# A transformer block with a mixture of experts: the third pair of expert weights is loaded behind the scatters, results are copied out later

## The chip, the cores and the metric

The kernel runs on one core of one Trainium2 chip. The metric is the device time of one execution, in microseconds (us), as the median of several runs. A profile of one execution tells what each engine and each transfer did.

## The reference

`x` has 4 sequences of 128 tokens of 512 numbers, so 512 tokens in all. Three parts are added to it one after the other: cross attention over 4 x 2048 context tokens, self attention, and the mixture of experts. Only the last one is touched here:

```python
logits = rn @ gate_w.T                       # rn: normalised tokens, 8 experts
probs = softmax(logits); rw, sel = top_k(probs, 2)
comb = sum(one_hot(sel, 8) * rw[..., None], axis=1)
h = gelu(einsum('nc,efc->enf', xf, w1))      # w1: 8 x 1024 x 512
y = einsum('enf,ecf->enc', h, w2)            # w2: 8 x 512 x 1024
out = einsum('enc,ne->nc', y, comb)
```

Each token needs two of the eight experts. The output is `x` plus this sum.

## The kernel before, in words

Cross attention takes the first two thirds of the time, self attention ends at about 809 us, and `mixture` does the rest.

**Tiles.** The 1024 pairs (token, expert) are sorted into tiles of 128 rows that belong to one expert each. There are 15 tiles (`TILES`): tile k below 8 has expert k, and the 7 further ones have the expert that the routing gives them (`of_tile`, read by `experts_of_further_tiles` on the sync engine, SP, by way of registers). Each tile loads its expert's two matrices anew, 2 MB each.

**Scatter of rows.** GpSimd (POOL) writes records of 514 numbers (512 of the normalised token, its weight, its token number) to the places of the sorted order in `slots_in` in HBM. These are 8 indirect DMAs (L1494): four from `t.normed` (first choices), four from `m_second` (second choices). Only when all 8 have landed (`sent`) may SP load tiles of rows back (`rows_load`, L1462). The first three tiles (`EARLY`) take their activations by another way, straight from SBUF (`rows_picked`), so they need no scatter, but the weight of a row, by which a result is scaled, comes with the loaded rows also for them.

**One tile k.** ScalarE (ACT) splits each f32 matrix into a high half in f16 (`w1_high` L1654, `w2_high` L1662, two instructions each), VectorE (DVE) makes the low half from the matrix and the high half, both in SBUF (`w1_low` L1622, `w2_low` L1629, two each). TensorE (PE) does `up` (L1797 to L1799, 96 products of 128x128), ACT applies Gelu (L1713) and splits (L1717), DVE makes the low half of that (L1638), PE does `down_tile` (L1779 to L1781, 24 products of 128x512), ACT scales the result into `y` (`y_evict`, L1680), and POOL adds `y` to the output by an indirect DMA with addition (L1504). POOL waits there for `y_out` of tile k and for the landing of the addition before it (`y_added`).

**Order of the work.** It is written out by hand, engine by engine. ACT in its iteration k: `y_evict(k - 2)`, Gelu and split of both halves of tile k, `x_high(k + 1)`, `w2_high(k)`, `w1_high(k + 2)`; after the last iteration the results of tiles 13 and 14. DVE in iteration k: `w1_low(k + 1)`, the low halves of tile k, `x_low(k + 1)`, `w2_low(k)`. PE: `up(k)`, transposes of the rows of k + 1, `down_tile(k - 1)`. SP's queue: `w1_load(2)`, `w1_load(3)`, `w2_load(2)`, the wait for `sent`, four `rows_load`, the experts of the further tiles, and then for each k `rows_load(k + 4)`, `w1_load(k + 3)`, `w2_load(k + 2)`.

**Buffers.** There are two buffers for each matrix (raw f32, high, low), so a matrix is loaded when the low half of the one two before it is done. `rows_in` is a ring of 8 (`ROWS_RING`); a slot comes free when the addition of its tile has landed. `y` has two buffers, `ps_y` (in PSUM) two.

Of the kernel before, what the change touches and what calls it, by code (L numbers as in the profile page):

```python
# [14 lines left out]
ALU, ACT, AX = mybir.AluOpType, mybir.ActivationFunctionType, mybir.AxisListType  # L15

P = 128
NB = 4
D = 512
# [1321 lines left out]
TILES = EXPERTS + MORE  # L1341
PARTS = 2
ROWS_AHEAD = 4
ROWS_RING = 8
RECORD = D + 2
EARLY = 3


def mixture(nc, io, t, s):
# [6 lines left out]
    with ExitStack() as ctx:  # L1356
        def sb(name, shape, dt=F32):
            return ctx.enter_context(nc.sbuf_tensor(name, shape, dt))

        def sem(name):  # L1360
            return ctx.enter_context(nc.semaphore(name))
# [5 lines left out]
                        for half in (t.cT_hi, t.cT_lo)]  # L1367
        rows_in = [sb(f"rows_in{u}", [P, RECORD]) for u in range(ROWS_RING)]
        xT_hi, xT_lo = [[sb(f"m_xT_{half}{u}", [P, NC, P], F16) for u in range(2)] for half in ("hi", "lo")]
        h_f = sb("h_f", [P, 2, NC, P])  # L1370
        h_hi, h_lo = [[sb(f"h_{half}{u}", [P, NF, P], F16) for u in range(2)] for half in ("hi", "lo")]
        y = [sb(f"m_y{u}", [P, D]) for u in range(2)]
        second = sb("m_second", [P, NB, RECORD])
        stats, mv, rstd = sb("m_stats", [P, 6]), sb("m_mv", [P, 2]), sb("m_rstd", [P, 2])
        hat = sb("m_hat", [P, D])
# [22 lines left out]
        ps_y = [ctx.enter_context(nc.psum_tensor(f"ps_y{i}", [P, D], F32)) for i in range(2)]  # L1398
# [8 lines left out]
        w1_in, w2_in = s.w1_in, s.w2_in  # L1407
        rows_got = [sem(f"rows_got{u}") for u in range(ROWS_RING)]
        w1_hi_s, w1_lo_s, w2_hi_s, w2_lo_s = s.w1_hi, s.w1_lo, sem("w2_hi_s"), sem("w2_lo_s")
# [3 lines left out]
        y_added, copied = sem("y_added"), sem("m_copied")  # L1413
# [11 lines left out]
        def w1_parts(k):  # L1425

            return NF + PARTS * k
# [5 lines left out]
        @block.sync  # L1433
        def _(sp):
            sp.dma_start(before[:, :, :], io.before).then_inc(const_in, 16)
            sp.dma_start(counting[:, :], io.counting).then_inc(const_in, 16)
            sp.dma_start(second[:, :, D + 1], io.tokens[:, 0:NB], allow_slow_non_contiguous=True).then_inc(s.tokens_in, 16)
            for b in range(NB):
                sp.dma_start(io.out[P * b:P * (b + 1), :], t.x[:, b, :]).then_inc(s.out_sem, 16)

            expert = list(range(EXPERTS))

            def experts_of_further_tiles():
                sp.wait_ge(rowed, 2)
                expert.extend(sp.value_load(of_tile[0:1, k:k + 1], min_val=0, max_val=EXPERTS - 1) for k in range(MORE))  # L1445

            def weights_of(w, k):
                e = expert[k]
                return (w[e:e + 1, :, :, :] if k < EXPERTS else w[bass.ds(e, 1), :, :, :]).rearrange("e p c n -> (e p) c n")

            def w1_load(k):
                sp.wait_ge(w1_lo_s, w1_parts(k - 2))
                sp.dma_start(w1_raw[k % 2][:, :, :], weights_of(io.w1, k)).then_inc(w1_in[k % 2], 16)

            def w2_load(k):
                sp.wait_ge(w2_lo_s, PARTS * (k - 1))
                sp.dma_start(w2_raw[k % 2][:, :, :], weights_of(io.w2, k)).then_inc(w2_in[k % 2], 16)

            def rows_load(k):
                if k >= ROWS_RING:  # L1460
                    sp.wait_ge(y_added, 16 * (k - ROWS_RING + 1))
                sp.dma_start(rows_in[k % ROWS_RING][:, :], io.slots_in[P * k:P * (k + 1), :]  # L1462
                             ).then_inc(rows_got[k % ROWS_RING], 16)

            w1_load(2)
            w1_load(3)
            w2_load(2)
            sp.wait_ge(sent, 16 * 2 * NB)
            for k in (*range(EARLY, ROWS_AHEAD), *range(EARLY)):
                rows_load(k)  # L1470
            experts_of_further_tiles()
            for k in range(TILES):
                if k + ROWS_AHEAD < TILES:
                    rows_load(k + ROWS_AHEAD)
                if 4 <= k + 3 < TILES:
                    w1_load(k + 3)
                if 3 <= k + 2 < TILES:
                    w2_load(k + 2)
            sp.wait_ge(y_added, 16 * TILES)

        @block.gpsimd
        def _(pool):
            mixture_deviations(nc, pool, t, s, NB - 1, mv, rstd)
            nc.gpsimd.memset(chosen[:, NB, :], 0.0).then_inc(const_in, 1)
            nc.gpsimd.memset(ones[:, :], 1.0).then_inc(const_in, 1)

            pool.wait_ge(s.slots_zeroed, 16)
            pool.wait_ge(rowed, 1)
            pool.wait_ge(s.tokens_in, 16 * 2)
            for k, records in enumerate((t.normed, second)):  # L1490
                for b in range(NB):
                    if k:
                        pool.wait_ge(copied, NB + b + 1)
                    nc.gpsimd.indirect_dma_start(  # L1494
                        out=io.slots_in, out_offset=bass.IndirectOffsetOnAxis(ap=rows[:, k, b:b + 1], axis=0),
                        in_=records[:, b, :], in_offset=None, bounds_check=TILES * P - 1).then_inc(sent, 16)

            pool.wait_ge(s.out_sem, 16 * (NB + 1))
            for k in range(TILES):
                pool.wait_ge(y_out, k + 1)  # L1500
                if k:
                    pool.wait_ge(y_added, 16 * k)
                token = rows_in[k % ROWS_RING][:, D + 1:D + 2].bitcast(mybir.dt.uint32)
                nc.gpsimd.indirect_dma_start(  # L1504
                    out=io.out, out_offset=bass.IndirectOffsetOnAxis(ap=token, axis=0), in_=y[k % 2][:, :],
                    in_offset=None, bounds_check=NB * P + P - 1, compute_op=ALU.add).then_inc(y_added, 16)

        @block.vector
        def _(v):
# [64 lines left out]
            def x_low(k):  # L1574
                if k < EARLY:
                    v.wait_ge(x_tr, k + 1)
# [56 lines left out]
            for k in range(TILES):  # L1633
                if k + 1 < TILES:
                    w1_low(k + 1)
                for i in range(2):
# [3 lines left out]
                                                   op0=ALU.mult, op1=ALU.subtract).then_inc(h_lo_s, 1)  # L1640
                    if i == (0 if k + 1 < EARLY else 1) and k + 1 < TILES:
                        x_low(k + 1)
                if k + 2 < EARLY:
                    pick_rows(k + 2)
# [3 lines left out]
        def _(act):  # L1648
# [8 lines left out]
            def w2_high(k):  # L1657
                act.wait_ge(w2_in[k % 2], 16 * uses(k))
                if k >= 2:
                    act.wait_ge(down, k - 1)  # L1660
                for i in range(PARTS):
                    nc.scalar.activation(w2_split(w2_hi[k % 2], i), w2_split(w2_raw[k % 2], i), ACT.Copy,  # L1662
                                         scale=W_SCALE).then_inc(w2_hi_s, 1)

            def x_high(k):
                act.wait_ge(x_tr, k + 1)
                if k < EARLY:
                    nc.scalar.activation(xT_hi[k % 2][:, :, :], ps_x[0][:, :].rearrange("p (c n) -> p c n", c=NC),
# [5 lines left out]
            def y_evict(k):  # L1674
                act.wait_ge(down, k + 1)
                if k < EARLY:
                    act.wait_ge(rows_got[k], 16)
                if k >= 2:
                    act.wait_ge(y_added, 16 * (k - 1))
                nc.scalar.activation(y[k % 2][:, :], ps_y[k % 2][:, :], ACT.Copy,  # L1680
                                     scale=rows_in[k % ROWS_RING][:, D:D + 1]).then_inc(y_out, 1)

            def rows_high(b):
# [20 lines left out]
                second_copy(b)  # L1704
            x_high(0)
            for k in range(TILES):
                if k >= 2:
                    y_evict(k - 2)
                for i in range(2):
                    act.wait_ge(up, 2 * k + i + 1)  # L1710
                    if k:
                        act.wait_ge(h_lo_s, 2 * (k - 1) + i + 1)
                    nc.scalar.activation(h_f[:, i, :, :], ps_h[i][:, :, :], ACT.Gelu, scale=UNSCALE).then_inc(gelu, 1)  # L1713
                    act.wait_ge(gelu, 2 * k + i + 1)
                    if k >= 2:
                        act.wait_ge(down, k - 1)
                    nc.scalar.activation(h_hi[k % 2][:, NC * i:NC * (i + 1), :], h_f[:, i, :, :], ACT.Copy,  # L1717
                                         scale=A_SCALE).then_inc(h_hi_s, 1)
                    if i == (0 if k + 1 < EARLY else 1) and k + 1 < TILES:
                        x_high(k + 1)  # L1720
                if k:
                    w2_high(k)
                if k + 2 < TILES:
                    w1_high(k + 2)
            y_evict(TILES - 2)
# [192 lines left out]
```

## Time and profile before

| | us |
|---|---|
| median of 3 runs | 1032.48 (1028.92 to 1034.45) |
| profiled execution, own time | 1033.27 |
| its span | 1031.5 |
| PE busy | 913.2 (89%) |
| DVE busy | 686.1 (67%) |
| ACT busy | 527.9 (51%) |
| POOL busy | 407.2 (39%) |

All times in the rows are microseconds from the start of the span. In a timeline a row gives start, busy time, engine, line and operation, what it writes and reads, how many instructions are merged, and in brackets how long the engine was idle before and what ended that. In a table of windows a row gives the stretch, its length, then busy time and number of instructions of PE, PEld (weight load), DVE, ACT and POOL, then the granted TensorE clock as a share of 2.4 GHz, the mean busy share of the 16 DMA engines (it can come out a little above 1), and GB/s. A row of DMA issues gives target and source, the queue, how many, KB of each, and the median time from issue to landing. In the tables the high and low halves of w1 are `w_hi` and `w_lo`, those of w2 are `cT_hi` and `cT_lo`, whose memory they use.

### The profile page before, as it was taken

The page shows a single profiled execution, that of the slowest core. Times are in us where ns is not written, and L with a number is a line of the kernel's source. Part 1 is how long each engine was busy: PE and PEld are TensorE (multiplying, and loading weights), DVE is VectorE, ACT ScalarE, POOL GpSimd, SP SyncE. Part 2 cuts the span into 40 slices and gives each one's busy share as a digit, 9 for nine tenths or more (in the row PEclk, how much of TensorE's full clock was granted, in tenths as well). Part 3 has the DMA queues.
Part 4 walks back from the last instruction along what each step waited for, and adds up shares of the span by engine and source line. Part 5 has one row for each costly group of instructions (what it writes and reads, how often), then busy time and mean ns, then how long its engine had stood idle before and what let it go on. Part 6 is the DMA issues. An engine that isn't in the chain of part 4 may idle for free. (4 is left out here: it accounts for less than half of the span.)

```text
span 1031.5 us, 24517 instructions
## 1 busy us (share of the span) xinstructions
PE 913.2 (89%) x10397; PEld 611.0 (59%) x10397; DVE 686.1 (67%) x1010; ACT 527.9 (51%) x801; POOL 407.2 (39%) x293
## 2 busy tenths in 40 slices
PE   5988999999999999999999999767775495899996
PEld 3464676676676676676676676433443383676663
DVE  7854777646777645777644455775667495799983
ACT  3543445555345545345544345531554562899893
POOL 2020665355665355665345545422230074111112
PEclk9998999999999999999999999669997597999999
DMA  9361122443022332022332022007600355999993
GB/s 340 103 180 42 33 61 60 126 105 89 22 59 63 124 105 54 20 56 63 124 106 53 22 54 62 2 1 263 270 2 1 129 212 171 414 400 398 400 391 45
DMA packets 48455, 134.63 MB, mean 131 GB/s; under 512 B 9870, under 2 KB 11790, under 8 KB 44506
## 3 DMA queue, kind: packets, MB, share of 16 engines
q1 hardware_dynamic: 45356, 126.78, 36.1%
q0 software_dynamic: 2800, 6.04, 2.9%
q8 instruction: 82, 1.34, 0.5%
q10 hardware_dynamic: 192, 0.26, 0.1%
q14 instruction: 25, 0.20, 0.1%
HBM read 94.99 MB, written 11.33 MB: 103 GB/s over the span
## 5 line engine op out<-in xcount | busy, mean ns | idle before, releaser
L419 POOL TENSOR_TENSOR acc_pool<-acc_pool,pT 128x1024 f32<-128x1024 f32 x92 | 216.7, 2355 | 170.2 <-ACT pT L688 168.5
L688 ACT ACTIVATE pT<-ps_s 128x1024 f32<-128x1024 f32 x128 | 130.7, 1021 | 216.7 <-PE ps_s L857 216.4
L526 DVE TENSOR_REDUCE mpart<-ps_b 128x1 f32<-128x512 f32 x256 | 174.4, 686 | 94.7 <-PE ps_b L835 93.6
L819 PE MATMUL ps_a<-wv_hi,cT_hi 128*128 128x128 f16 x1024 | 184.4, 220 | 0.4 <-ACT kbias L608 0.4
L821 PE MATMUL ps_a<-wv_hi,cT_lo 128*128 128x128 f16 x1024 | 183.3, 219 | 0.0
L820 PE MATMUL ps_a<-wv_lo,cT_hi 128*128 128x128 f16 x1024 | 183.2, 219 | 0.0
L521 DVE TENSOR_TENSOR k_lo<-k_f,k_hi 128x512 f16<-128x512 f32 x64 | 72.3, 1129 | 70.2 <-ACT k_hi L664 69.9
L835 PE MATMUL ps_b<-k_stack,q_stack 98*128 98x512 f16 x256 | 98.6, 388 | 11.9 <-DVE mpart L526 7.7
L819 PEld LDWEIGHTS ps_a<-wv_hi,cT_hi 128*128 128x128 f16 x1024 | 99.7, 97 | 12.4 <-issue 11.9
L857 PE MATMUL ps_s<-q_stack,k_stack 98*128 98x128 f16 x1024 | 100.2, 227 | 7.3 <-ACT pT L688 6.2
L820 PEld LDWEIGHTS ps_a<-wv_lo,cT_hi 128*128 128x128 f16 x1024 | 100.2, 98 | 5.0
L857 PEld LDWEIGHTS ps_s<-q_stack,k_stack 98*128 98x128 f16 x1024 | 75.8, 101 | 45.7 <-ACT pT L688 15.6
L821 PEld LDWEIGHTS ps_a<-wv_hi,cT_lo 128*128 128x128 f16 x1024 | 99.7, 97 | 0.0
L801 PE MATMUL ps_a<-cT_hi,wk_hi 128*128 128x512 f16 x256 | 98.9, 386 | 0.0
L802 PE MATMUL ps_a<-cT_lo,wk_hi 128*128 128x512 f16 x256 | 97.7, 382 | 0.0
L803 PE MATMUL ps_a<-cT_hi,wk_lo 128*128 128x512 f16 x256 | 97.7, 381 | 0.0
L1797 PE MATMUL ps_h<-m_xT_hi,w_hi 128*128 128x128 f16 x480 | 81.2, 219 | 10.4 <-issue 5.7
L871 PE MATMUL ps_o<-pT,vals 128*32 128x128 f32 x2048 | 87.2, 289 | 0.1
L1504 POOL DMA_INDIRECT out<-m_y,rows_in x15 | 27.9, 1861 | 138.2 <-DMA out<-m_y,rows_in 105.3
L1799 PE MATMUL ps_h<-m_xT_hi,w_lo 128*128 128x128 f16 x480 | 81.3, 219 | 0.0
L1798 PE MATMUL ps_h<-m_xT_lo,w_hi 128*128 128x128 f16 x480 | 81.2, 219 | 0.0
L514 DVE TENSOR_TENSOR cT_lo<-ps_b,cT_hi 128x512 f16<-128x512 f32 x64 | 43.8, 689 | 52.7 <-ACT cT_hi L627 52.7
(248 smaller groups left out, 1873.9 us busy)
## 6 DMA issues: line engine op xcount, KB each, us to landing
w_raw<-in_w SPq DMA_DIRECT2D x30, 2048.0 KB, 16.8
raw<-in_context SPq DMA_DIRECT2D x16, 1024.0 KB, 5.8
k_stack<-k_hi SPq DMA_DIRECT2D x252, 64.0 KB, 2.0
k_stack<-k_lo SPq DMA_DIRECT2D x128, 64.0 KB, 2.0
slots_in<-a_zeros SPq DMA_DIRECT2D x1, 3855.0 KB, 13.6
rows_in<-slots_in SPq DMA_DIRECT2D x15, 257.0 KB, 16.3
q_stack<-k_stack SPq DMA_DIRECT2D x12, 128.0 KB, 2.4
x_sb<-in_x SPq DMA_DIRECT2D x2, 512.0 KB, 4.1
```

The lines of the kernel that those rows point to most:

```text
L419: nc.gpsimd.tensor_tensor(acc_pool[:, :], pT[:, 0, :] if p == 1 else acc_pool[:, :], pT[:, p % PT, :], ALU.add).then_inc(pool_add, 1)
L526: nc.vector.tensor_reduce(mpart[:, j, kb:kb + 1], bank_b(step)[:, :], AX.X, ALU.max).then_inc(p1_max, 1)
L688: nc.scalar.activation(pT[:, p % PT, :], ps_s[:, :], ACT.Exp, scale=SM_SCALE).then_inc(exp_done, 1)
L801: nc.tensor.matmul(bank[:, :], t.wk_hi[:, c, col], cT_hi[:, c, keys], start=(c == 0), stop=False)
L802: nc.tensor.matmul(bank[:, :], t.wk_hi[:, c, col], cT_lo[:, c, keys], start=False, stop=False)
L803: last = nc.tensor.matmul(bank[:, :], t.wk_lo[:, c, col], cT_hi[:, c, keys], start=False, stop=(c == NC - 1))
L819: nc.tensor.matmul(to, cT_hi[:, c, keys], t.wv_hi[:, c, col], start=(c == 0), stop=False)
L820: nc.tensor.matmul(to, cT_hi[:, c, keys], t.wv_lo[:, c, col], start=False, stop=False)
L821: last = nc.tensor.matmul(to, cT_lo[:, c, keys], t.wv_hi[:, c, col], start=False, stop=(c == NC - 1))
L835: nc.tensor.matmul(bank[:, :], t.q_stack[0:ROWS, HPG * g + j, b * P:(b + 1) * P], t.k_stack[w % 2][0:ROWS, j, KB * kb:KB * (kb + 1)], star ...
L857: last = nc.tensor.matmul(ps_s[:, at:at + P], t.k_stack[w % 2][0:ROWS, j, P * kt:P * (kt + 1)], t.q_stack[0:ROWS, HPG * g + j, b * P:(b + ...
L871: last = nc.tensor.matmul(ps_o[w % 2][HD * j:HD * (j + 1), 0:P], vals[w % 2][:, 2 * p + i, HD * j:HD * (j + 1)], pT[:, p % PT, at:at + P], ...
```

## The change

On SP, `w1_load(3)` and `w2_load(2)` move from ahead of the wait for `sent` to behind the four first `rows_load`. On ACT, `y_evict(k - 2)` moves from the head of iteration k to behind `w2_high(k)`, ahead of `w1_high(k + 2)`. `y` gets a third buffer, so an eviction waits for the addition three tiles back and no longer two. For the memory, the ring of rows shrinks from 8 to 7, so `rows_load(k)` waits for the addition of tile k - 7 and no longer k - 8.

```diff
-ROWS_RING = 8
+ROWS_RING = 7
+Y_RING = 3
...
-        y = [sb(f"m_y{u}", [P, D]) for u in range(2)]
+        y = [sb(f"m_y{u}", [P, D]) for u in range(Y_RING)]
...
             w1_load(2)
-            w1_load(3)
-            w2_load(2)
             sp.wait_ge(sent, 16 * 2 * NB)
             for k in (*range(EARLY, ROWS_AHEAD), *range(EARLY)):
                 rows_load(k)
+            w1_load(3)
+            w2_load(2)
             experts_of_further_tiles()
...
-                    out=io.out, out_offset=bass.IndirectOffsetOnAxis(ap=token, axis=0), in_=y[k % 2][:, :],
+                    out=io.out, out_offset=bass.IndirectOffsetOnAxis(ap=token, axis=0), in_=y[k % Y_RING][:, :],
...
-                if k >= 2:
-                    act.wait_ge(y_added, 16 * (k - 1))
-                nc.scalar.activation(y[k % 2][:, :], ps_y[k % 2][:, :], ACT.Copy,
+                if k >= Y_RING:
+                    act.wait_ge(y_added, 16 * (k - Y_RING + 1))
+                nc.scalar.activation(y[k % Y_RING][:, :], ps_y[k % 2][:, :], ACT.Copy,
...
             for k in range(TILES):
-                if k >= 2:
-                    y_evict(k - 2)
                 for i in range(2):
...
                 if k:
                     w2_high(k)
+                if k >= 2:
+                    y_evict(k - 2)
                 if k + 2 < TILES:
                     w1_high(k + 2)
```

## Rows read from the trace of the kernel before

**Rows 1.** Windows of the mixture, core 0: quiet stretch, first row loads, steady tiles.
```profile
852.00:858.50 6.50, 1.69 (x31) 1.51 (x28) 5.40 (x3) 0.00 (x0) 6.24 (x1) 0.91 0.00 0
...
863.00:869.50 6.50, 3.92 (x12) 1.96 (x13) 1.06 (x2) 3.32 (x7) 1.58 (x1) 0.50 0.51 167
...
902.00:972.00 70.00, 66.51 (x742) 48.09 (x740) 64.50 (x42) 63.60 (x60) 11.63 (x6) 1.00 1.02 401
```

**Rows 2.** Timeline of POOL, three of the eight scatters.
```profile
838.34 9.89 POOL L1494 DMA_INDIRECT slots_in<-m_second,m_rows  x1 [0.30 <-issue]
848.53 9.71 POOL L1494 DMA_INDIRECT slots_in<-m_second,m_rows  x1 [0.30 <-issue]
...
859.82 0.97 POOL L1494 DMA_INDIRECT slots_in<-m_second,m_rows  x1 [0.30 <-issue]
```

**Rows 3.** Timeline of DVE beside these scatters.
```profile
847.30 0.69 DVE L1577 CAST m_xT_lo<-ps_x 128x512 f16<-128x512 f32 x1
...
848.50 4.49 DVE L1629 SCALAR_TENSOR_TENSOR cT_lo<-w_raw,cT_hi 128x2048 f16<-128x2048 f32 x2
852.90 4.49 DVE L1622 SCALAR_TENSOR_TENSOR w_lo<-w_raw,w_hi 128x2048 f16<-128x2048 f32 x2
```

**Rows 4.** Timeline of SP's queue: release by the scatters, first weight load behind it.
```profile
862.61 6.75 SPq L1462 DMA_DIRECT2D rows_in<-slots_in  x6
869.40 0.43 SPq L1453 DMA_DIRECT2D w_raw<-in_w  x1
```

**Rows 5.** DMA issues in 868 to 869.8: the load issued at 869.40.
```profile
w_raw<-in_w SPq DMA_DIRECT2D x1, 2048.0 KB, 9.1
```

**Rows 6.** DMA issues in 862 to 863.2: the first two row loads.
```profile
rows_in<-slots_in SPq DMA_DIRECT2D x2, 257.0 KB, 2.9
```

**Rows 7.** Timeline of ACT: eviction of tile 0, then one steady tile.
```profile
866.12 0.69 ACT L1680 ACTIVATE m_y<-ps_y,rows_in 128x512 f32<-128x512 f32 x1 [14.47 <-DMA rows_in<-slots_in]
...
929.23 0.67 ACT L1680 ACTIVATE m_y<-ps_y,rows_in 128x512 f32<-128x512 f32 x1
...
932.57 3.70 ACT L1662 ACTIVATE cT_hi<-w_raw 128x2048 f16<-128x2048 f32 x2
937.33 3.71 ACT L1654 ACTIVATE w_hi<-w_raw 128x2048 f16<-128x2048 f32 x2 [1.06 <-DMA w_raw<-in_w]
```

**Rows 8.** Timeline of SP's queue in the same steady tile.
```profile
939.02 0.33 SPq L1457 DMA_DIRECT2D w_raw<-in_w  x1
...
943.93 0.33 SPq L1453 DMA_DIRECT2D w_raw<-in_w  x1
```

**Rows 9.** DMA issues in 939 to 939.3: that w2 load.
```profile
w_raw<-in_w SPq DMA_DIRECT2D x1, 2048.0 KB, 16.1
```

**Rows 10.** Timeline of DVE in the same steady tile.
```profile
934.50 4.49 DVE L1629 SCALAR_TENSOR_TENSOR cT_lo<-w_raw,cT_hi 128x2048 f16<-128x2048 f32 x2 [0.66 <-ACT cT_hi L1662]
939.27 4.50 DVE L1622 SCALAR_TENSOR_TENSOR w_lo<-w_raw,w_hi 128x2048 f16<-128x2048 f32 x2 [0.28 <-ACT w_hi L1654]
```

**Rows 11.** Timeline of POOL: a steady addition, and the last two.
```profile
944.38 2.00 POOL L1504 DMA_INDIRECT out<-m_y,rows_in  x1 [9.73 <-DMA out<-m_y,rows_in]
...
1017.54 2.35 POOL L1504 DMA_INDIRECT out<-m_y,rows_in  x1 [6.10 <-ACT m_y L1680]
1025.43 1.54 POOL L1504 DMA_INDIRECT out<-m_y,rows_in  x1 [5.54 <-ACT m_y L1680]
```

**Rows 12.** DMA issues in 932 to 934: an addition under full load.
```profile
out<-m_y,rows_in POOLq DMA_INDIRECT x1, 10.9
```

**Rows 13.** DMA issues in 1009 to 1012: the addition issued at 1009.90.
```profile
out<-m_y,rows_in POOLq DMA_INDIRECT x1, 4.3
```

**Rows 14.** DMA issues in 1017 to 1019: the addition issued at 1017.54.
```profile
out<-m_y,rows_in POOLq DMA_INDIRECT x1, 5.5
```

**Rows 15.** Timelines of ACT and DVE: the last w2 split.
```profile
1012.06 3.69 ACT L1662 ACTIVATE cT_hi<-w_raw 128x2048 f16<-128x2048 f32 x2
...
1013.98 4.49 DVE L1629 SCALAR_TENSOR_TENSOR cT_lo<-w_raw,cT_hi 128x2048 f16<-128x2048 f32 x2 [1.11 <-ACT cT_hi L1662]
```

## The prediction, on record before the changed kernel ran

> **What bounds the kernel now.** I read the windows of the mixture first, then the timelines of POOL, DVE, SP and ACT, and last the times from issue to landing. In the steady tiles, 902 to 972 us, the DMA engines are full (share 1.02, 401 GB/s) while PE is busy 66.51 of 70 us [rows 1]. A tile takes 11.73 us: the addition at 944.38 begins 9.73 + 2.00 us after the one before it began [rows 11]. ACT waits 1.06 us per tile for w1 [rows 7], and a w2 load lands 16.1 us after its issue [rows 9], that is, nearly three loads of 2.1 MB stand in the queue (5.2 us each at 401 GB/s). So transfers set the pace. Before that there is a hole: in 852 to 858.5 the DMA share is 0.00 [rows 1], because SP waits for the scatters. They end at 862.61, when SP issues the first row loads; w1 of tile 4 goes out only at 869.40 [rows 4]. After 1006 the weights are all in, and the end is set by PE, `down_tile(14)`, the last eviction and the last addition.
>
> **Part 1, what slows the scatters.** Two of the eight take 9.89 and 9.71 us, the last one 0.97 [rows 2]. Two explanations are open, and the change bets on one: that the two weight loads in flight slow them. The second scatter ends at 858.24, after 6 us without any transfer [rows 1]. DVE splits weights without a gap from 848.50 to 857.39 [rows 3]; the scatter ends 0.85 us after that, about its own 0.97 us. The scatter before it ends at 848.23, which is 0.93 us after DVE began, at 847.30, the one instruction of that stretch that reads PSUM and not two operands in SBUF [rows 2, 3]. Both ends follow DVE, none a transfer. So POOL is shut out while DVE reads two SBUF operands.
>
> The Trainium skill, "SBUF — State Buffer", section "Who interferes with whom", says that a DVE instruction with two SBUF inputs contends with a GpSimd instruction that reads SBUF; the two rows agree. The same section infers that such an instruction does not hold up the generation of descriptors; by that the weights' traffic would be the culprit, which is rival C below.
>
> What does the change do to this? w1(3) is not loaded yet, so DVE has no w1 split of tile 3 to do at 852.90 [rows 3]. It falls silent at 852.99, the sixth scatter ends at 852.99 + 0.85 = 853.84, the two others follow with 0.30 + 0.97 us each [rows 2], so the last starts at 855.4, and lands as before after 862.61 - 859.82 = 2.8 us. Release: 858.2 us, 4.4 earlier. Ends: 844.9 (both slow ones at 0.97) and 862.6 (nothing gained). I take 858.2.
>
> **Part 2, the two moved loads.** They were carried ahead of the hole, and now go behind the row loads. From the release the queue must carry, before w1(4) is in: six row loads (6 x 0.263 MB), w1(3), w2(2) and w1(4) (3 x 2.097 MB), 7.87 MB, 19.6 us at 401 GB/s [rows 1]. To this comes the delay of a queue that starts empty: two row loads need 1.3 us by that rate and landed after 2.9 [rows 6], so 1.6; the load issued at 869.40 had two row loads ahead of it, 2.63 MB or 6.5 us, and landed after 9.1 [rows 5], so 2.6. w1(4) lands at 858.2 + 19.6 + 1.6 to 2.6 = 879.4 to 880.4, before at 878.5. SP's own issue is no limit: reading the experts and two row loads took SP from 862.61 to 869.40, 6.8 us [rows 4], and is done at about 866 beside these transfers. So the stream of weights, whose total is unchanged, runs 0.9 to 1.9 us later from there to its end. I take 1.1, nearer the lower end because row loads head the queue. The hole at 852 is closed at its end but widened at its start.
>
> On ACT `w1_high(3)` now waits for w1(3) (landing about 868.5), with Gelu of tile 2 queued behind it; before, `y_evict(0)` blocked ACT until 866.12 in the same way [rows 7]. DVE and PE wait with it: ACT's first half takes 1.85 us, DVE's two 4.49, the small low halves behind them about 2, so tile 3's products start at about 876.8. By the same steps from w1(4)'s landing tile 4's start at about 888.5. PE has 11.7 us in between for what keeps it busy for 11.1 at the full clock (66.51 us in 70 us, six tiles) [rows 1]. Its clock was at 0.50, that is 1.2 GHz, behind its pause [rows 1], and will be again, which costs it some us that later tiles give back, since they wait for weights. Cost 0; if nothing hides it, up to 3 us.
>
> **Part 3, the eviction behind w2.** In steady tiles ACT waits 1.06 us for w1 after `w2_high`; the 0.67 us of `y_evict` now stand in that gap and no longer ahead of Gelu [rows 7]. Gain nothing and cost nothing, since transfers set the pace. But the result is ready later: w2's split now ends at 932.57 - 0.67 + 3.70 = 935.6, the eviction at 936.2, before at 929.90. POOL can start at about 937, in the middle of DVE's w2 split, which by then runs from 933.9 to 938.3 [rows 10]. It gets in between this and the w1 split at 939.27, and ends near 938.3 + 1.5 = 939.8. Before, it ended at 944.38 - 9.73 = 934.65 [rows 11] and landed 10.9 us after its issue at 932.65 [rows 12], 8.9 us after its end. So it lands at 948.7.
>
> **Part 4, the ring of 7.** `rows_load(k + 4)` now waits for the addition of tile k - 3, which is just this one, and `w1_load(k + 3)` and `w2_load(k + 2)` stand behind it on SP. The w1 load moves from 943.93 [rows 8] to 949.1. What hides it is the depth of the queue: the w2 load issued at 939.02 lands 16.1 us later [rows 8, 9], at 955.1, so 6 us of work remain, and a new load needs a lead of 1.6 to 2.6 us. Cost 0, with 3.4 us of reserve; without it see rival B.
>
> **Part 5, the end.** Nothing on PE's way to its last product changes: `down_tile(14)` waits for the low half of w2(14), done at 1013.98 + 4.49 = 1018.47 [rows 15]. But the result of tile 12 now leaves ACT after `w2_high(14)`: 1012.06 + 3.69 + 0.6 = 1016.3 [rows 15]. Its addition starts at about 1017.1, in the place that tile 13's has now (1017.54, with the same wait for DVE until 1018.4), and lands like that one, 5.5 us after 1017.54 [rows 11, 14], at 1023.0. POOL takes 0.8 us from a landing to the next start (944.38 - 932.65 - 10.9). Tile 13's starts at 1023.9, lands after 4.3 us [rows 13] at 1028.2, and tile 14's starts at 1029.0 in place of 1025.43 [rows 11]: 3.6 us later, and 4.8 if tile 13's takes 5.5 too. I take 3.7. If tile 12's result left as early as now, it would be 0. The additions run one after another, and three are now left at the end where there were two.
>
> **Sum.** 1.1 + 3.7 = 4.8 us. The profiled execution took 1033.27 us, 0.8 above the median of 1032.48, so the same work comes to 1038.1 on its own scale and 1037.3 on the median's. With its bounds (0.9 to 1.9, up to 3 if PE's delay isn't hidden, 3.6 to 4.8) and the spread of the runs shown, about 1034 to 1042. Only over 0.5%, 5.2 us, can this kernel be told from no change: slower begins at 1037.6.
>
> **Rivals.**
> *B, SP's wait starves the queue.* If an addition lands more than about 0.8 us later than in part 3, the next POOL start misses the gap before DVE's w1 split, and waits for its end at 939.27 + 4.50 = 943.77 [rows 10]. It then ends at 945.3 and lands at 954.2, the next w1 load can't be moving before 956.2 to 957.2, and the queue ran dry at 955.1: 1 to 2 us lost in each turn of three tiles, and more as the loads behind it bunch. With 0.6 us per tile over some 10 tiles, 6 us more: 1043. For it: the gap is short and the landing times under load vary. Against: a later landing also moves the w1 split later, which widens the gap.
> *C, the scatters were slowed by the weights.* Then both take 0.97 us, the release comes at 844.9, 13.3 us before that of part 1, and the sum is 4.8 - 13.3 = -8.5: 1024, faster. It decides if the sixth scatter takes about 1 us though DVE is splitting. For it: by SP's order w1(3) and w2(2) are issued before the release, beside the scatters. Against: the ends of both, above.
> *D, the added parts cancel.* The copy's removal from the head of ACT's list lets Gelu start 0.67 us earlier in every tile; where a tile is set by this chain and not by the transfer (the early tiles and the last three), some 4 us come back: 1033.5. For it: ACT's and DVE's rows have gaps of hardly over 1 us [rows 7, 10]. Against: ACT's 1.06 us of waiting per tile.
>
> **Chances.** The forecast 0.50, B 0.20, D 0.18, C 0.12. The forecast lies at the bound: 0.23 of it slower, 0.27 the same. Slower: 0.23 + 0.19 of B = 0.42. Faster: 0.12 of C and 0.02 of D's lower end = 0.14. Same: the rest, 0.44. The range leaves out C and the upper end of B: 1030 to 1045.
>
> **What would show it.** Part 1: scatters five and six at 9.9 and about 5.3 us, row loads at 858.2. Part 2: w1(4) split at about 880 on ACT. Parts 3 and 4: additions start at a landing, w1 loads right behind a row load, DMA share still 1.0 in steady tiles; a share below 0.97 there speaks for B. Part 5: the last three additions about 5 us apart, the last at 1030 or so. Wrong would make it: scatters that end while DVE still splits, or a release before 850.

## The result, and the profile after

The changed kernel takes 1050.86 us in the median of 4 runs (1040.81 to 1052.96); the kernel before took 1030.70 beside it (1027.71 to 1034.45). The ratio is 1.0174, 95% interval 1.0098 to 1.0251: slower, beyond the 0.5% that the prediction set as its bound, and above its range of 1030 to 1045. Whether it is 2% slower these four runs leave open. The profiled execution took 1052.96 us with a span of 1051.0; that of before had a span of 1031.5.

Where the 19.5 us arose is read from five instants that both traces have. First those of before that no group above holds: the first instruction of the mixture on VectorE, and the high halves of w1 of tiles 4 and 14 on ScalarE.

```profile
809.18 0.69 DVE L1519 BATCH_NORM_STATS2 m_stats<-x_sb 128x6 f32<-128x512 f32 x1 [0.32 <-PEq L921]
...
878.56 3.71 ACT L1654 ACTIVATE w_hi<-w_raw 128x2048 f16<-128x2048 f32 x2 [5.38 <-DMA w_raw<-in_w]
...
996.61 3.71 ACT L1654 ACTIVATE w_hi<-w_raw 128x2048 f16<-128x2048 f32 x2 [0.31 <-DMA w_raw<-in_w]
```

The same three in the changed kernel, with the first row loads on SP between them:

```profile
806.96 0.69 DVE L1520 BATCH_NORM_STATS2 m_stats<-x_sb 128x6 f32<-128x512 f32 x1 [0.32 <-PEq L921]
...
856.26 1.75 SPq L1463 DMA_DIRECT2D rows_in<-slots_in  x4
...
878.47 3.71 ACT L1655 ACTIVATE w_hi<-w_raw 128x2048 f16<-128x2048 f32 x2 [0.51 <-DMA w_raw<-in_w]
...
1011.93 3.71 ACT L1655 ACTIVATE w_hi<-w_raw 128x2048 f16<-128x2048 f32 x2 [0.62 <-DMA w_raw<-in_w]
```

| stretch | before, us | after, us | difference |
|---|---|---|---|
| up to the mixture | 809.2 | 807.0 | -2.2 |
| to the first row loads | 53.4 | 49.3 | -4.1 |
| to the high half of w1(4) | 15.9 | 22.2 | +6.3 |
| to that of w1(14) | 118.1 | 133.5 | +15.4 |
| to the end of the span | 34.9 | 39.1 | +4.2 |

The first row lies ahead of everything that the change touches; its 2.2 us are a difference between two executions. The three stretches that the forecast had a sum for came out near it. The steady tiles, which it put down at nothing, hold 15.4 us.

**The scatters.** POOL's timeline of the changed kernel, answering to [rows 2]: the fifth, sixth and last scatter.

```profile
836.35 9.89 POOL L1495 DMA_INDIRECT slots_in<-m_second,m_rows  x1 [0.30 <-issue]
846.54 5.30 POOL L1495 DMA_INDIRECT slots_in<-m_second,m_rows  x1 [0.30 <-issue]
...
853.42 0.98 POOL L1495 DMA_INDIRECT slots_in<-m_second,m_rows  x1 [0.30 <-issue]
```

The windows answering to [rows 1]; columns as there.

```profile
834.00:852.00 18.00, 17.77 (x248) 14.68 (x245) 16.49 (x14) 10.50 (x10) 16.93 (x4) 1.00 0.16 58
852.00:858.50 6.50, 0.00 (x0) 0.00 (x0) 0.00 (x0) 0.00 (x0) 1.95 (x2) 0.77 0.49 162
...
902.00:972.00 70.00, 61.77 (x680) 46.57 (x677) 54.58 (x36) 52.86 (x50) 12.67 (x5) 0.95 0.91 334
```

The DMA engines are nearly empty (0.16) while the fifth scatter takes its 9.89 us again. This speaks against the weights' traffic as what holds it; the run with VectorE's wait, below, decides. The sixth is shorter by just the two splits that VectorE no longer has to do there.

**The steady tiles.** They move 334 GB/s in place of 401, the DMA share falls from 1.02 to 0.91, and PE's busy time from 66.51 to 61.77 of 70 us. SP's queue, answering to [rows 8]:

```profile
948.12 0.33 SPq L1463 DMA_DIRECT2D rows_in<-slots_in  x1
948.64 0.33 SPq L1454 DMA_DIRECT2D w_raw<-in_w  x1
949.08 0.37 SPq L1458 DMA_DIRECT2D w_raw<-in_w  x1
963.23 0.33 SPq L1463 DMA_DIRECT2D rows_in<-slots_in  x1
```

A row load, both weight loads, then nothing for 14 us. The chain of waits in this stretch (start, length, what) says what SP and POOL wait for:

```profile
935.22 12.88 DMA out<-m_y,rows_in
...
948.22 0.72 issue
948.94 14.27 DMA out<-m_y,rows_in
...
963.32 0.72 issue
964.04 13.06 DMA out<-m_y,rows_in
```

One addition after another, 12.9 to 14.3 us each here, where it was 10.9 [rows 12], and at each landing SP sends its three loads. Windows of one such turn:

```profile
949.00:955.00 6.00, 3.31 (x52) 2.75 (x50) 5.60 (x6) 5.76 (x6) 2.88 (x1) 1.00 1.02 382
955.00:961.50 6.50, 6.50 (x72) 4.71 (x70) 4.30 (x2) 4.10 (x4) 0.00 (x0) 1.00 1.00 366
961.50:964.00 2.50, 2.02 (x10) 0.69 (x8) 2.50 (x3) 2.44 (x6) 0.00 (x0) 1.00 0.09 33
```

The queue is full until 961.5 and then dry (0.09) until the next landing at 963.2 releases the next three. That is the dry queue of rival B, but with all loads bunched. By windows of half a microsecond the dry stretch is 1.0 to 2.5 us in the other turns, and 0.5 us in the one whose landing came at 948.10.

**The end.** The last three additions, answering to [rows 11]:

```profile
1033.07 2.79 POOL L1505 DMA_INDIRECT out<-m_y,rows_in  x1 [6.37 <-ACT m_y L1681]
1039.92 1.54 POOL L1505 DMA_INDIRECT out<-m_y,rows_in  x1 [4.07 <-DMA out<-m_y,rows_in]
1045.41 1.54 POOL L1505 DMA_INDIRECT out<-m_y,rows_in  x1 [3.95 <-DMA out<-m_y,rows_in]
```

The last one now waits for a landing and no longer for ScalarE.

### The profile page after: what moved, and what is told of

It is laid out like the page before. It is cut to its first block and busy times, and to the rows that moved or that the text cites. A ratio compares the mean times of both kernels' runs of the same rounds, so it can differ in the third digit from the quotient of the medians.

```text
span 1051.0 us, 24517 instructions
## 1 busy us (share of the span) xinstructions
PE 916.6 (87%) x10397; PEld 617.6 (59%) x10397; DVE 686.3 (65%) x1010; ACT 528.4 (50%) x801; POOL 408.9 (39%) x293
## 2 busy tenths in 40 slices
DMA packets 48455, 134.63 MB, mean 128 GB/s; under 512 B 9870, under 2 KB 11790, under 8 KB 44506
## 5 line engine op out<-in xcount | busy, mean ns | idle before, releaser
L688 ACT ACTIVATE pT<-ps_s 128x1024 f32<-128x1024 f32 x128 | 130.8, 1022 | 216.3 <-PE ps_s L857 216.1
L1798 PE MATMUL ps_h<-m_xT_hi,w_hi 128*128 128x128 f16 x480 | 88.6, 229 | 26.7 <-DVE m_xT_lo L1582 24.4
L819 PEld LDWEIGHTS ps_a<-wv_hi,cT_hi 128*128 128x128 f16 x1024 | 99.8, 97 | 12.4 <-issue 11.9
L857 PEld LDWEIGHTS ps_s<-q_stack,k_stack 98*128 98x128 f16 x1024 | 75.0, 100 | 45.8 <-ACT pT L688 15.9
L1505 POOL DMA_INDIRECT out<-m_y,rows_in x15 | 33.8, 2251 | 158.8 <-DMA out<-m_y,rows_in 127.9
L1623 DVE SCALAR_TENSOR_TENSOR w_lo<-w_raw,w_hi 128x2048 f16<-128x2048 f32 x28 | 62.9, 2287 | 42.6 <-ACT w_hi L1655 42.6
L1799 PE MATMUL ps_h<-m_xT_lo,w_hi 128*128 128x128 f16 x480 | 88.6, 229 | 0.0
L1800 PE MATMUL ps_h<-m_xT_hi,w_lo 128*128 128x128 f16 x480 | 88.5, 229 | 0.0
```

Of the source, the lines that this page charges most:

```text
L688: nc.scalar.activation(pT[:, p % PT, :], ps_s[:, :], ACT.Exp, scale=SM_SCALE).then_inc(exp_done, 1)
L819: nc.tensor.matmul(to, cT_hi[:, c, keys], t.wv_hi[:, c, col], start=(c == 0), stop=False)
L857: last = nc.tensor.matmul(ps_s[:, at:at + P], t.k_stack[w % 2][0:ROWS, j, P * kt:P * (kt + 1)], t.q_stack[0:ROWS, HPG * g + j, b * P:(b + ...
L1798: nc.tensor.matmul(to, w1_hi[u][:, c, col], xT_hi[u][:, c, :], start=(c == 0), stop=False)
```

## The experiments

All ratios are to the kernel before, run beside each on the same chip. That kernel itself spreads from about 1022 to 1039 us; a likely reason stands below, with what is not shown of it. A period is the distance of the high halves of w1.

**Loads moved alone.** The kernel before with this edit:

```diff
             w1_load(2)
-            w1_load(3)
-            w2_load(2)
             sp.wait_ge(sent, 16 * 2 * NB)
             for k in (*range(EARLY, ROWS_AHEAD), *range(EARLY)):
                 rows_load(k)
+            w1_load(3)
+            w2_load(2)
```

> Only the two weight loads move behind the scatters; eviction, y buffers and the ring of 8 rows stay as before. Theory Q (the ring of 7 together with the late copy puts SP's weight loads behind an addition, and that paces the steady tiles): steady period stays 11.7 us, time of before + 1 to 3 us, about 1032 to 1034. Rival L (the moved loads themselves do the harm): 10 us or more slower, about 1042.

1028.07 us, ratio 0.9968 (0.9925 to 1.0010): no harm and no gain to be told, where 1 to 3 us of harm were expected. Steady tiles 11.7 us. In this profile no scatter took over 2.9 us, as told below. Rival L falls.

**Late copy, third y buffer and ring of 7 alone,** the edit above taken back from the changed kernel.

> The loads go back ahead of the scatters; late copy, 3 y buffers and the ring of 7 stay as in the changed kernel. Theory Q: period of the steady tiles 13.5 to 14.3 us, sum 14 to 20 us over before, about 1045 to 1050. Rival L: like before, within 4 us.

1049.33 us, ratio 1.0185 (1.0095 to 1.0276), as much as the whole change. The window 902 to 972 of its trace:

```profile
902.00:972.00 70.00, 61.32 (x633) 44.87 (x632) 55.74 (x38) 54.97 (x53) 11.88 (x5) 0.95 0.90 330
```

**The changed kernel with the ring at 8,** and for the memory with two `y` buffers.

```diff
-ROWS_RING = 7
+ROWS_RING = 8
-Y_RING = 3
+Y_RING = 2
```

> The changed kernel with the ring of rows at 8 again (y back at 2 buffers, for the memory). rows_load(k + 4) waits again for the addition four tiles back. Theory Q: the gap closes, steady period 11.7 us, time of before + 4 to 6 us (stream 1.1, end 3.7), about 1036. Rival P (the additions, one after another at 13 to 14 us each, set the pace by themselves once the copy is late): still 12 us or more slower.

1042.05 us, ratio 1.0110 (1.0023 to 1.0196). The steady tiles are whole again, in the same window:

```profile
902.00:972.00 70.00, 68.82 (x761) 49.86 (x758) 64.88 (x43) 63.44 (x61) 10.43 (x6) 1.00 1.02 400
```

From w1(14) to the end it takes 38.6 us (before 34.9): the late copy's cost at the end remains. The total is higher than the 1036 expected, with few runs and a wide interval. Rival P falls: with the copy late and this ring, the additions run at 11.7 us. The first landings here are just as slow as in the changed kernel (13.7, 12.3 and 12.3 us, against 13.4, 12.8 and 14.0), but then they settle at 10.9, and those of the changed kernel do not. The edit also takes back the third `y` buffer; that this buffer does no harm is shown by the next run, which keeps it.

**The changed kernel with SP's row load behind the weights.**

```diff
             for k in range(TILES):
-                if k + ROWS_AHEAD < TILES:
-                    rows_load(k + ROWS_AHEAD)
                 if 4 <= k + 3 < TILES:
                     w1_load(k + 3)
                 if 3 <= k + 2 < TILES:
                     w2_load(k + 2)
+                if k + ROWS_AHEAD < TILES:
+                    rows_load(k + ROWS_AHEAD)
```

> The changed kernel, but in SP's loop the row load stands behind the two weight loads of its iteration and no longer ahead of them, so a weight load waits for the addition one iteration earlier. Ring 7, 3 y buffers, late copy stay. Theory Q: weights no longer wait long for an addition, steady period 11.7 to 12.2 us, about 1036 to 1040. Rival P: 13.5 us or more per tile and about 1050, since the additions are unchanged.

1039.02 us, ratio 1.0050 (0.9999 to 1.0101). Nothing but the order of three issues on one queue differs from the changed kernel. Its window, two row loads with the weight loads between them on SP, and an addition's landing time:

```profile
902.00:972.00 70.00, 69.63 (x786) 51.33 (x784) 65.17 (x43) 64.30 (x61) 11.59 (x6) 1.00 1.02 399
```

```profile
933.00 0.33 SPq L1463 DMA_DIRECT2D rows_in<-slots_in  x1
933.52 0.33 SPq L1454 DMA_DIRECT2D w_raw<-in_w  x1
939.53 0.33 SPq L1458 DMA_DIRECT2D w_raw<-in_w  x1
944.72 0.33 SPq L1463 DMA_DIRECT2D rows_in<-slots_in  x1
```

```profile
out<-m_y,rows_in POOLq DMA_INDIRECT x1, 10.9
```

Row loads still wait for an addition here, but the w1 load behind it is only delayed to 933.5, and the w2 load goes out by itself 6 us later, when its buffer is free. The loads are spread again, and the addition again lands after 10.9 us. In the profiles, from the mixture's first instruction to the end, this run and the one with the ring at 8 take 226.9 and 227.0 us, the kernel before 222.3: 4.6 and 4.7 us more, as the forecast's 4.8 without a loss in the steady tiles.

**The ring of 7 alone,** in the kernel before.

> The kernel before with the ring of rows at 7 and nothing else (copy early, 2 y buffers). Theory Q: it takes ring and late copy together, since with the early copy the addition of tile k - 3 lands about when the w1 load goes out anyway; within 2 us of before, period 11.7 us. Rival R (the ring alone does it): period 13 us or more, 1045 us.

1031.06 us, ratio 1.0014 (0.9974 to 1.0053), steady tiles of 11.7 us: no difference that can be told. Rival R falls.

**The early copy in the changed kernel,** that is, `y_evict(k - 2)` back at the head of ScalarE's iteration, all else as changed.

> The changed kernel with the eviction back at the head of ScalarE's iteration; ring 7, 3 y buffers and the moved loads stay. Theory Q: period 11.7 us, end of the last w1 split to end of the span 34 to 35 us and no longer 38 to 39, time as with the moved loads alone, 1026 to 1032. If the ring of 7 or the third buffer did it without the late copy: period 13 us or more.

1035.35 us, ratio 1.0064 (1.0023 to 1.0106), steady tiles of 11.7 us and 36.2 us from w1(14) to the end. So the loss in the steady tiles takes the late copy and the ring of 7 together. The time is 3 us above what was expected at most, and the end 1.3 us longer; the fifth and sixth scatter took 9.89 and 5.30 us in this profile, as in the changed kernel, but whether that is all of it stays open.

**The changed kernel with weights in halves.** Each weight load becomes two DMAs, so the packets are half as large (48455 packets in the trace of the changed kernel, 52200 here, for the same bytes):

```diff
-                sp.dma_start(w1_raw[k % 2][:, :, :], weights_of(io.w1, k)).then_inc(w1_in[k % 2], 16)
+                for i in range(2):
+                    sp.dma_start(w1_raw[k % 2][:, 2 * i:2 * i + 2, :], weights_of(io.w1, k)[:, 2 * i:2 * i + 2, :]
+                                 ).then_inc(w1_in[k % 2], 16)
```

and in the same way for w2, with the waits adapted.

> The changed kernel with each weight load split into two DMAs of half the columns, so that a packet has 8 KB and no longer 16 KB. Theory S (an addition lands late because its 2 KB packets take turns with 16 KB packets): additions land 2 us sooner, period 12 to 13 us in place of 14, time 5 to 12 us under the changed kernel. Without that share in it: period 14 us, time as the changed kernel.

1036.31 us, ratio 1.0058 (1.0015 to 1.0101), by the two ratios some 12 us under the changed kernel, with its ring, its late copy and its order untouched. A tile takes 11.9 us, a little less than expected. Its window, and an addition's landing (12.7 to 14.3 in the steady tiles of the changed kernel, 10.6 to 11.1 in those of this run):

```profile
902.00:972.00 70.00, 66.06 (x736) 47.65 (x735) 63.72 (x42) 61.15 (x60) 15.46 (x6) 1.00 1.03 397
```

```profile
out<-m_y,rows_in POOLq DMA_INDIRECT x1, 11.1
```

So the loop hangs on the size of the packets that an addition shares the DMA engines with. How much of the 2 to 3 us is the size itself is another matter, since w2 loads also go out less bunched here, 1.6 to 2.4 us behind w1 in place of 0.4 to 1.2. The last two runs below differ in the halves alone and have spread loads: there a steady addition lands after 10.9 us with 16 KB packets and 10.5 with 8 KB, or 9.0 and 7.7 us after the end of POOL's instruction. The Trainium skill, "DMA: Bandwidth & Descriptors", section "Queues, rings and completion order", says that a DMA engine takes turns between its queues packet by packet. The landing times move the way that this rule has it, but in that pair by far less than the packets shrink.

**VectorE waits until the scatters are issued.** In the kernel before:

```diff
+            nc.gpsimd.memset(mark[:, :], 0.0).then_inc(const_in, 1)    # POOL, behind the eight scatters
...
+                if k == 0:
+                    v.wait_ge(const_in, 16 * 2 + 3)                    # VectorE
                 w2_low(k)
```

> The kernel before, but VectorE waits ahead of the low half of w2 of tile 0 until GpSimd has issued all eight scatters (a small memset behind them tells it). Theory V (VectorE's splits shut GpSimd out, not the weights' traffic): all eight scatters take about 1 us each, though the weights are loaded early; row loads 8 to 15 us earlier than in the profile of before, and a time of about 1022 to 1025 in every run instead of 1023 to 1039. Rival W (traffic of the weights slows the scatters' instructions): two of them still near 10 us, time as before.

1023.04 us, ratio 0.9953 (0.9922 to 0.9984), runs from 1018.5 to 1027.0. The same three scatters as above and the mark:

```profile
834.46 0.97 POOL L1495 DMA_INDIRECT slots_in<-m_second,m_rows  x1 [0.30 <-issue]
835.74 0.97 POOL L1495 DMA_INDIRECT slots_in<-m_second,m_rows  x1 [0.30 <-issue]
...
838.34 0.97 POOL L1495 DMA_INDIRECT slots_in<-m_second,m_rows  x1 [0.30 <-issue]
839.30 0.12 POOL L1498 MEMSET m_mark<- 128x1 f32 x1
```

With w1(3) in flight, at a DMA share of 0.95 in 834 to 839, each takes 0.97 us. So rival W falls, and with it rival C of the prediction. The first two of these rows would have been quick without the wait too, since VectorE paused by itself before 835.90, for 3.96 us. What VectorE's wait does is seen at the last scatter, in two runs with the loads moved and with nearly the same pause of VectorE (3.98 and 4.00 us): the changed kernel in halves, without the wait, and then the changed kernel with the wait, further below.

```profile
841.80 9.30 POOL L1499 DMA_INDIRECT slots_in<-m_second,m_rows  x1 [0.30 <-issue]
```

```profile
843.00 0.97 POOL L1496 DMA_INDIRECT slots_in<-m_second,m_rows  x1 [0.30 <-issue]
```

The DMA share is 0.08 beside the slow one (841.8 to 851) and 0.57 beside the quick one (841.6 to 844). In all five profiles with the wait the scatters take 0.97 to 1.04 us from the third on; theory V holds. Its "in every run" was too bold, since the runs reach 1027.0.

**The same wait with the two loads moved.**

> The same wait of VectorE, and in addition the two weight loads behind the scatters. Theory V: scatters about 1 us each as in the run beside it, their landing some 5 us sooner because no weights are in flight, but w1 of tile 4 no earlier than there: within 3 us of it. Rival W: this one is clearly faster than the one beside it, by 8 us or more.

1025.74 us, ratio 0.9976 (0.9941 to 1.0011). The row loads come 36.4 us after the mixture's start in place of 40.0, the high half of w1(4) at 60.7 in place of 57.6. So even with free scatters moving the loads loses 3.1 us at w1(4), where it gains 3.6 at the release. The total isn't clearly faster, so rival W falls here too.

**The same wait in the changed kernel.**

> The changed kernel in full, plus VectorE's wait until the scatters are issued. Theory Q: row loads come at about 36 us from the start of the mixture as in the run of the moved loads with that wait, but the steady tiles still take 14 us, so 12 to 20 us slower than the kernel before with the same wait (1023): 1035 to 1043. If the loss of the changed kernel were one of its start, it would be gone here: 1026.

1040.97 us, ratio 1.0136 (1.0070 to 1.0202). The start is as early as in the run before this one (36.2 us), the window isn't:

```profile
902.00:972.00 70.00, 61.07 (x646) 45.94 (x644) 55.17 (x36) 54.33 (x52) 11.81 (x5) 0.93 0.93 340
```

**Two tries for more speed.** Both have VectorE's wait in the kernel before, and SP reads the experts of the further tiles ahead of iteration 4 of its loop and not ahead of iteration 0. The second also has the weights in halves.

> The kernel before with VectorE's wait, and SP reads the experts of the further tiles only ahead of its fifth iteration, not ahead of the first. Bottleneck theory (the stream of weights sets the pace from its first load on): w1 of tile 4 goes out 4 us sooner, 2 to 4 us faster than the run with the wait alone, 1019 to 1021. If the early loads are not what the rest waits for: like it, 1023.

> As the run beside it, and the weights loaded in halves (8 KB packets). Additions land sooner, but with the early copy nobody waits for them in the steady tiles, so the period stays near 11.7 and the time within 3 us of the run beside it, unless the additions are what holds the end.

1023.39 us, ratio 0.9944 (0.9905 to 0.9983), and 1023.63, ratio 0.9938 (0.9902 to 0.9975). Neither can be told from the run with the wait alone. The first missed what was expected of it: the high half of w1(4) came at 57.8 us of the mixture in place of 57.6, so SP's reading of the experts had been hidden. The kernel before with VectorE's wait beats both kernels, by about 0.5% the one before.

## Why the prediction was wrong

**Part 1, the scatters: right.** The sixth took 5.30 us (about 5.3 forecast), the fifth 9.89, the release came 4.1 us sooner (4.4). That VectorE shuts POOL out, and not the traffic, is shown by the runs in which VectorE waits. What I missed is that it differs from one execution to the next. In the profile with the loads moved alone the same instructions of POOL met a pause of VectorE:

```profile
836.90 0.97 POOL L1494 DMA_INDIRECT slots_in<-m_second,m_rows  x1 [0.30 <-issue]
838.18 0.98 POOL L1494 DMA_INDIRECT slots_in<-m_second,m_rows  x1 [0.31 <-issue]
839.46 2.22 POOL L1494 DMA_INDIRECT slots_in<-m_second,m_rows  x1 [0.30 <-issue]
841.98 1.90 POOL L1494 DMA_INDIRECT slots_in<-m_second,m_rows  x1 [0.30 <-issue]
```

VectorE's pause there and in the kernel before, then the window 826 to 830 of the trace with the loads moved and 827 to 830 of the kernel before:

```profile
837.14 0.69 DVE L1638 SCALAR_TENSOR_TENSOR h_lo<-h_f,h_hi 128x512 f16<-128x512 f32 x1 [2.75 <-ACT h_hi L1717]
```

```profile
836.50 0.69 DVE L1638 SCALAR_TENSOR_TENSOR h_lo<-h_f,h_hi 128x512 f16<-128x512 f32 x1 [0.76 <-ACT h_hi L1717]
```

```profile
826.00:830.00 4.00, 3.49 (x34) 3.52 (x35) 3.69 (x15) 1.52 (x2) 0.77 (x1) 0.50 0.01 2
```

```profile
827.00:830.00 3.00, 2.13 (x39) 2.17 (x40) 2.62 (x14) 1.88 (x2) 0.00 (x0) 1.00 0.00 0
```

TensorE was still at 0.50 (1.2 GHz) there, in the profile of before at 1.00 (2.4 GHz), though it had paused for the same 4.4 us before this work in both. TensorE gets through fewer products at 0.50 (34 in 4 us against 39 in 3), and VectorE waits 2.75 us in place of 0.76. The fifth and sixth scatter fall into this pause, and the last one starts 34.4 us from the mixture's start in place of 50.6. The late copy alone, with the loads where before has them, met the same, and its row loads came 8 us earlier than in the profile of before (45.3 for 53.4). But a pause of this length isn't enough by itself: with the ring at 8 VectorE paused for 2.81 us, the fifth and sixth scatter took 1 us, and the seventh and eighth 9.48 and 5.30, where with the loads moved alone they got in after 2.22 and 1.90. What decides between these is not shown, nor why the clock rose sooner in some executions. That the spread of the kernel before (1022 to 1039) comes from this is argued from a few profiles of each kind. The spread of ten runs speaks for it only weakly: 7 to 12 us in the four sets with the wait outside the changed kernel, 11 to 16 us in five sets without it.

**Part 2, the moved loads: right in kind, about 1 us too small.** From the release to w1(4) 22.2 us, where the forecast took 21.4 (879.6 - 858.2) and had 22.2 at the upper end of its range. The net of parts 1 and 2 is +2.1 us in the profiles, 1.1 forecast and 1.9 at most; the run that moves only the loads shows no loss that can be measured. No run shows a cost of the delay on PE.

**Part 3, the addition's landing: the step that failed.** I said "so it lands at 948.7", by a landing 8.9 us after POOL's end, the figure of a kernel whose loads go out one by one. Measured are 12.7 to 14.3 us from issue to landing in place of 10.9. In the turn shown, from POOL's end at 951.88 to the landing at 963.21 it is 11.3, not 8.9. I took as a constant what depends on the order of the loads that the change alters. And the forecast's own figures had no room for it: POOL's start at about 937, a landing at 948.7 and 0.8 us to the next start make 12.5 us from one addition to the next, longer than a tile of 11.73. In the kernel before 10.9 and 0.8 fill the tile exactly. I never held this chain against the period.

**Part 4, "cost 0, with 3.4 us of reserve": failed with it.** I followed one w1 load past the ring's wait and held it against a queue as deep as in the kernel before. But once SP stands at an addition's landing, the w2 load behind it is late as well, and both leave together. Then each turn is: landing, 0.8 us, the addition's instruction of 2 to 3 us, and a landing that in the turn shown comes at 963.21, after the queue has run empty at 961.5. That makes 14 us, with 0.5 to 2.5 us of a dry queue in a turn. The reserve was counted once for a loop that turns in every tile. The experiments take the loop apart in four ways: the ring at 8, the row load behind the weights, the copy early, or smaller packets each bring back 11.7 to 11.9 us per tile, at DMA shares of 1.02 or 1.03.

Rival B named this place and the queue that runs dry, with a chance of 0.20 and a price of 0.6 us per tile. The mechanism is B's, the price is not: over the ten tiles from w1(4) to w1(14) the period is 13.35 us in place of 11.81, 1.5 more on average, and once the loop has closed it is 14.1, 2.3 more. I had priced one late load per turn of three tiles; it is three late loads in each tile. B's trigger was also another one, not the gap ahead of the w1 split but the bunching: the addition at 948.94 came while VectorE was on its w1 split (945.97 to 950.46), and lost 1.4 us there of its 2.94, less than B gave for a missed gap.

**Part 5, the end: right.** 4.2 us measured, 3.7 forecast (3.6 to 4.8). In all five other kernels with the late copy it is 38.2 to 38.8 us from w1(14) to the end against 34.9.

Rivals C and D didn't occur. The forecast put part 4 at nothing and summed to 4.8 us; parts 1, 2 and 5 alone come to 6.3 in the profiles, and the steady tiles add the 15.4 that it lacked.

## What to carry to other kernels

When an edit puts a queue behind the end of a chain, don't ask whether one transfer still comes in time; ask what is issued together once the queue has waited the first time, and follow the loop until it repeats. Here the smaller ring alone and the later producer with the larger ring both left the steady tiles at 11.7 us, and together they made them 14, so add up their dependences in tiles: rows of k + 4 wait on the addition of k - 3, whose result had just been moved half a tile back. And before transfers are blamed for a slow instruction, look at what ends beside it.

## What the runs showed of the hardware that I had not expected

- A scatter of 128 records took 0.97 us alone and 9.89 us beside VectorE's back-to-back instructions with two operands in SBUF, in which it passed over four of their borders; at another border, 832.45 in the changed kernel, it got in. What decides this stays open.
- An addition of 128 rows of 2 KB, at full DMA load, took 10.9 us to land among spread loads with 16 KB packets and 12.7 to 14.3 among bunched ones; with 8 KB packets 10.5 among spread loads and 10.6 to 11.1 in the changed kernel.
- Where all scatters were quick, weights in flight delayed the landing of the scatters, though not their instructions: from the last scatter's start to the row loads 10.9 us with them (846.00 to 856.86, late copy alone) and 4.5 without (841.98 to 846.45, loads alone).
